# First feed-forward started inside the end of the first attention

## The reference

```python
h = _L0_tok_ref(x, ...)
h = h + _L0_attn_ref(_layernorm(h), wq, wk, wv, wo)      # 16 heads of 64, causal
h = h + _L0_ffn_ref(_layernorm(h), w1, b1, w2, b2)       # 256 -> 1024 -> 256
h = h + _L1_attn_ref(_layernorm(h), Wq, Wk, Wv, Wo, bo)
h = h + _L1_ffn_ref(_layernorm(h), gate_weight, ...)     # 8 experts, all dense
```

```python
h = float2fix(jnp.einsum('bsd,df->bsf', x, w1) + b1, 8)
xq = float2fix(h, 8)
y = jnp.interp(xq, _PWL_X, _PWL_Y)       # 33 points on [-4, 4], GELU exact there
out = jnp.einsum('bsf,fd->bsd', float2fix(y, 8), w2) + b2
return float2fix(out, 8)
```

## Time and profile before

| what | value |
|---|---|
| median of 3 runs | 980.0 us (979.19 to 980.0) |
| profiled execution | 979.99 us, span 978.2 us |
| PE busy | 933.1 us (95%) |
| DVE busy | 579.8 us (59%) |
| ACT busy | 542.0 us (55%) |
| feed-forward of layer 0, first up block to last down projection | 238.3 to 318.7 us |

### The profile page before, as it was taken

How to read it: one execution, slowest core, us unless ns; L and a number is a source line. 1 busy time by engine, 2 the same in 40 slices (tenths; PEclk the granted TensorE clock), 3 DMA queues, 4 the chain that set the end, 5 groups by cost and what they waited for, 6 DMA issues and landing times.

```text
span 978.2 us, 18614 instructions
## 1 busy us (share of the span) xinstructions
PE 933.1 (95%) x7135; PEld 863.7 (88%) x7135; DVE 579.8 (59%) x1251; ACT 542.0 (55%) x1569; POOL 154.8 (16%) x173
## 2 busy tenths in 40 slices
PE   6999999999799999999999899999999999999998
PEld 6877888788677878888889898999999999999998
DVE  5566575746999574665656677555453545444342
ACT  4666464653764664655555526556664647555452
POOL 0332121210000122221210000431110111110111
PEclk9999999999999999999999999999999999999999
DMA  8310000002000210000002011111011111100001
GB/s 325 130 44 2 1 1 1 2 1 87 1 1 1 87 44 1 2 2 1 2 7 81 15 73 44 44 43 46 2 44 44 44 44 44 44 1 1 1 14 38
DMA packets 8796, 34.46 MB, mean 35 GB/s; under 512 B 642, under 2 KB 5122, under 8 KB 5380
## 3 DMA queue, kind: packets, MB, share of 16 engines
q1 hardware_dynamic: 8708, 33.28, 9.4%
HBM read 32.06 MB, written 1.22 MB: 34 GB/s over the span
## 4 chain that ended last, share of the span: by engine, by line
issue 32%; PE 24%; POOL 5%; DVE 5%; ACT 2%; POOLq 0%; DVEq 0%; ACTq 0%
PE D L574 8%; PE O L574 7%; POOL h L362 4%; PE O L740 2%; PE T L726 2%; PE S L715 1%; PE S L574 1%; DVE hid L1528 1%; ACT hid L1100 1%; DVE wslot L1128 1%; PE S L709 1%; POOL h L374 1%; ACT work L1096 1%; PE O L854 1%; POOL vbuf L372 1%
## 5 line engine op out<-in xcount | busy, mean ns | idle before, releaser
L1528 DVE TENSOR_TENSOR hid<-work,hid 128x300 fp32r<-128x300 f32 (+1 forms) x256 | 139.1, 565 | 191.9 <-ACT hid L1100 191.6
L574 PE MATMUL O<-hid,wslot 128*128 128x300 f32 (+3 forms) x1680 | 240.6, 301 | 0.0
L574 PEld LDWEIGHTS O<-hid,wslot 128*128 128x128 f32 x1680 | 233.0, 189 | 0.6
L574 PE MATMUL D<-xn,wslot 128*128 128x300 f32 (+3 forms) x1368 | 222.4, 307 | 1.4 <-ACT hid L1100 1.4
L574 PEld LDWEIGHTS D<-xn,wslot 128*128 128x128 f32 x1368 | 197.7, 189 | 6.1 <-ACT hid L1100 2.7
L1096 ACT ACTIVATE work<-D,prm 128x300 f32<-128x300 f32 (+1 forms) x128 | 66.7, 521 | 179.7 <-PE D L574 179.7
L996 ACT ACTIVATE probs<-S,negmax 111x111 f32<-111x111 f32 (+1 forms) x352 | 117.5, 358 | 53.5 <-DVE negmax L1293 53.2
L553 POOL TENSOR_TENSOR probs<-probs,rsum 111x444 f32<-111x444 f32 (+1 forms) x88 | 80.9, 920 | 379.8 <-DVE rsum L1301 379.8
L574 PE MATMUL S<-xn,wslot 128*128 128x300 f32 (+3 forms) x864 | 136.2, 305 | 0.0
L574 PEld LDWEIGHTS S<-xn,wslot 128*128 128x128 f32 x864 | 125.3, 191 | 0.3
L362 POOL TENSOR_TENSOR h<-h,work 128x300 f32<-128x300 f32 (+1 forms) x56 | 49.5, 905 | 287.6 <-DVE work L1547 287.6
(11 more groups left out here) (174 smaller groups left out, 1165.0 us busy)
## 6 DMA issues: line engine op xcount, KB each, us to landing
raw<-in_moe SPq DMA_DIRECT2D x16, 1024.0 KB, 4.8
raw<-in_attn SPq DMA_DIRECT2D x7, 1024.0 KB, 4.9
work<-in_x SPq DMA_DIRECT2D x2, 1008.0 KB, 8.0
w2f<-in_attn SPq DMA_DIRECT2D x1, 1024.0 KB, 12.6
raw<-in_ffn SPq DMA_DIRECT2D x1, 1024.0 KB, 4.8
w2f<-in_ffn SPq DMA_DIRECT2D x1, 1024.0 KB, 4.9
raw<-in_x SPq DMA_DIRECT2D x2, 504.0 KB, 5.2
out<-h SPq DMA_DIRECT2D x3, 300.0 KB, 2.8
```

The source lines that it names most:

```text
L574: mm = pe.matmul(psum, a, b, start=(first and k == 0), stop=(k == 3 * n - 1))
L1528: nc.vector.tensor_tensor(moe_hid(s, 1), moe_g(s)[:, 0:w], moe_hid(s, 0).bitcast(F32), ALU.subtract).then_inc(m_hid, 1)
```

## The change

TensorE: up blocks 0 and 1 take the places of `keep_busy` in step 22, blocks 2 and 3 that in step 23. Blocks 4 and 5 stand between the two halves of chunk 3's output projection, whose second half now goes to bank T0. The banks of the blocks turn S0, S1, D0, D1 (`BF`). The rest of the blocks follow, with mean and variance of chunk 3 behind blocks 7 and 12, and each half of a down projection by itself behind one pair or more. VectorE: `ff_find(0)` and `ff_part(0)` come in step 22; in the loop `ff_round` is done one pair later; the norm of chunk 3 is centred at p = 3 and finished at p = 9; evictions come by halves. Two quarter splits of each of two weight pieces move. ScalarE: `ff_load` of pair 0 in step 22, and two table loads more, for the root at p = 7.

```diff
+        BF = BS + BD
@@ attention, TensorE
+                    if (l, c, dc) == (0, NC - 1, KD - 1):
+                        pe.wait_ge(t_dve[0], 2 * NUNIT)
+                    else:
+                        take_bank("out", KD * c + dc)
...
                     if u == NUNIT:
-                        keep_busy(*ahead, 6)
+                        if l == 0:
+                            ff_up1(0)
+                        else:
+                            keep_busy(*ahead, 6)
                     if 0 <= u - 1 < NUNIT:
                         transposes(2 * u - 1)
                     if u == NUNIT + 1:
-                        keep_busy(*ahead, 5)
+                        if l == 0:
+                            ff_up1(2)
+                            ff_up1(3)
+                        else:
+                            keep_busy(*ahead, 5)
+                    elif u == NUNIT and l == 0:
+                        ff_up1(1)
...
+                    if l == 0 and u == NUNIT + 1:
+                        ff_up1(4)
+                        ff_up1(5)
                     if due is not None:
                         project_out(due, 1)
@@ feed-forward, TensorE
+            for s in range(6, NC * KH):
+                c, m = s // KH, s % KH
+                ff_up1(s)
+                if (c, m) == (0, KH - 1):
+                    mean(1, 3)
+                if (c, m) == (1, 4):
+                    variance(1, 3)
+                if c >= 1 and m == 5:
+                    ff_down(c - 1, 0)
+                if c >= 2 and m == 1:
+                    ff_down(c - 2, 1)
+                if (c, m) == (NC - 1, 3):
+                    mean(2, 0)
+            variance(2, 0)
+            ff_down(NC - 2, 1)
+            for dc in range(KD):
+                ff_down(NC - 1, dc)
@@ ScalarE
+                    if l == 0 and u == NUNIT:
+                        nc.scalar.preload_act_table_set("gelu_and_others")
+                        ff_load(0)
+                        ff_load(1)
...
+            for p in range(NP):
+                ff_knots(p)
                 if p + 1 < NP:
                     ff_load(2 * p + 2)
                     ff_load(2 * p + 3)
-                if p == -1:
+                if p == 3:
                     square(1, 3)
+                if p == 7:
+                    nc.scalar.preload_act_table_set("natural_log_exp_and_others")
                     inv_root(1, 3)
+                    nc.scalar.preload_act_table_set("gelu_and_others")
@@ VectorE
+                    if l == 0 and NUNIT - 2 <= u < NUNIT:
+                        low_quarter(FIRST_W + W_FF, 3 * (u - (NUNIT - 2)))
                     if u < NUNIT:
                         invert_sums(2 * u)
...
+            for p in range(1, NP + 2):
+                if p <= NP:
                     ff_slope(p - 1)
+                if p >= 2:
+                    ff_round(p - 2)
                 if p < NP:
                     ff_find(p)
+                if p <= NP:
                     ff_line(p - 1)
                 if p < NP:
                     ff_part(p)
+                if p <= NP:
                     ff_sum(p - 1)
-                    ff_round(p - 1)
-                if p == 0:
+                if p == 1:
+                    low_quarter(FIRST_W + 6, 2)
+                    low_quarter(FIRST_W + 6, 3)
+                if p in (1, 2):
+                    add_out(NC - 1, p - 1)
+                if p == 3:
                     center(1, 3)
+                if p == 9:
                     finish(1, 3)
-                if KH <= p < NP and p % (KH // 2) == 0:
-                    ff_out(2 * p // KH - 2)
+                if p in (7, 11, 15):
+                    ff_out1(p // 4 - 1, 0)
+                if p in (10, 14):
+                    ff_out1(p // 4 - 2, 1)
                 if p == 3 * KH // 2:
                     center(2, 0)
-            finish(2, 0)
-            ff_out(NC - 2)
+            root = newton(2, 0)
+            ff_out1(NC - 2, 1)
+            apply(2, 0, root)
             for k in range(SPLITS):
                 low_quarter(FIRST_W + 7, k)
-            ff_out(NC - 1)
+            for dc in range(KD):
+                ff_out1(NC - 1, dc)
```

More of the change, by code:

```diff
@@ L341, in ff_bufs @@
             if p % 3 == 0:
-                flat = vbuf[:, :, :].rearrange("p s n -> p (s n)")
-                three = [pair(flat, k) for k in range(3)]
+                three = [ffs[:, 2 * k:2 * k + 2, :] for k in range(3)]
             elif p % 3 == 1:
@@ L347, in ff_bufs @@
             else:
-                three = [ffs[:, 2 * k:2 * k + 2, :] for k in range(3)]
+                flat = vbuf[:, :, :].rearrange("p s n -> p (s n)")
+                three = [pair(flat, k) for k in range(3)]
             return [t[:, :, 0:w] for t in three]
@@ L813, in _ @@
             attention(0, 0)
[L816 to L834, removed]
-                    if c == 0 and m == 3:
-                        variance(1, 3)
-                    if c >= 2 and m == 1:
-                        ff_down(c - 2)
-                    if c == 2 and m == KH - 1:
-                        mean(2, 0)
-                    if c == NC - 1 and m == KH - 2:
-                        variance(2, 0)
@@ L844, in ff_down @@
-            def ff_down(c):
-                a, w = CHUNKS[c]
-                pe.wait_ge(ff_hid, KH * (c + 1))
-                if c == 0:
-                    pe.wait_ge(w2_in, 16)
-                for dc in range(KD):
-                    if c >= 1:
-                        pe.wait_ge(ff2_ev, KD * (c - 1) + dc + 1)
-                    w2 = w2f[:, :].rearrange("p (a n) -> p a n", n=D)
-                    for i in range(KH):
-                        mm = pe.matmul(BO[dc][:, 0:w], w2[:, i, dc * P:(dc + 1) * P],
-                                       work[:, KH * (c % 2) + i, 0:w], start=(i == 0), stop=(i == KH - 1))
-                    mm.then_inc(ff2_mm, 1)
@@ L1037, in _ @@
             high_part(FIRST_W + 2)
-            attention(0)
             def ff_load(s):
@@ L1056, in ff_knots @@
                 nc.scalar.activation(y1, y1, ACT.Gelu, bias=c_knot1[:, 0:1], scale=1.0 / UNIT).then_inc(ff_y1, 1)
-            for p in range(-1, NP):
-                if p >= 0:
-                    ff_knots(p)
+            attention(0)
+            for p in range(NP):
+                ff_knots(p)
                 if p + 1 < NP:
@@ L1353, in attention @@
                         invert_sums(2 * u + 1)
+                    if l == 0 and u == NUNIT + 1:
+                        break
                     if due is not None:
@@ L1363, in attention @@
                         low_out(u - 1)
+                    if l == 0 and u == NUNIT:
+                        ff_find(0)
+                        ff_part(0)
                     if l == 1 and u == NUNIT + 1:
```

72 lines of the change are left out of this document (47 added, 25 removed).

## The result

| | median us | lowest to highest | executions |
|---|---|---|---|
| before | 980.0 | 979.19 to 981.09 | 4 |
| after | 969.96 | 968.87 to 970.49 | 4 |

The ratio is 0.9895, 95% interval 0.9878 to 0.9913. The forecast was 970.2 us, faster than before.

A forecast was written before the change was run, and what follows sets the result against it. The prediction took VectorE's queue to bound the changed stretch and added its terms: -7.05 up to the last rounding and -2.7 in the tail, -9.8 from 979.99, giving 970.2 us, range 966.8 to 974.3.

The forecast's parts named there:

- The seam (-6.9, +0.3, -1.2): Attention end to feed-forward: VectorE's waits hidden -6.9, first wait grows to 0.9 us, +0.3, two quarter splits moved under cover -1.2.
- One pair, rounding later (-2.8): Feed-forward loop: rounding one pair later makes a wide pair 3.57 instead of 3.76 us; 15 pairs, -2.8 us.
- Rival 2: TensorE becomes the bound; 3 to 5 us of its pauses exposed give 973 to 975 us; chance 0.12.
- the sum for TensorE's queue: TensorE's work after 226.7 us: 73 us, ending at 299.5 without a pause, 7.7 us before the last down projection's forecast end.
- The new waits (+1.1, +0.55, +0.75): Loop: VectorE waits for the last chunk's root +1.1, down projection 0's half +0.55, a half ahead of blocks 30 and 31 +0.75.
- an unbroken chain: VectorE before the change: five waits at the seam, 0.38 to 2.38 us, then work without a break.
- rival 6: Slower through the clock: TensorE at 0.50 after a pause; one episode nothing to 1 us more, seven give 981; chance 0.04.
- Up to the last rounding: All terms from 226.7 us to the feed-forward's last rounding: -7.05 us, so it starts at 301.7 instead of 308.8.
- The tail (-4.4, +1.7): After the last rounding: last down projection waits less, -4.4; third block of the next layer waits for bank O1, +1.7.
- The half eviction (+1.15): VectorE: one half of chunk 2's evictions now stands before the last rounding, +1.15 us.
- The sum: Whole kernel: -7.05 up to the last rounding and -2.7 in the tail, -9.8 us, giving 970.2 us.
- sign of being wrong by the clock: Profile after: the prediction is wrong if the granted clock is 0.5 for more than one episode.

The follow-up runs named there:

- Kernel 10: Changed kernel with up blocks 0 to 5 started late again, VectorE's first find and part behind normalisation, splits and additions; 975.98 us, ratio 0.9952.
- kernel 1: Changed kernel with each rounding put back right behind its own sum; 970.51 us, ratio 0.9899 against the kernel before.
- kernel 2: Kernel before the change with only the rounding done one pair later; 980.0 us, ratio 0.9992.
- kernel 6: Changed kernel with the four quarter splits of the key weights behind chunk 3's evictions; 969.58 us, ratio 0.9897 against the kernel before.
- kernel 5: Changed kernel without the two table loads in the loop, chunk 3's root replaced by a scaled copy; 968.7 us, ratio 0.9893 against the kernel before.
- kernel 9: Changed kernel with six products of constants in TensorE's pause before chunk 3's mean; 969.23 us, ratio 0.9886 against the kernel before.
- kernel 12: Changed kernel with key-weight splits behind chunk 3's evictions, down projection 2's first half behind the last up block, six constant products in TensorE's pause; 968.05 us.
- kernel 4: Changed kernel with down projections whole again and each chunk's evictions together; 970.79 us, ratio 0.9899 against the kernel before.
- kernel 7: Kernel before the change with only chunk 2's evictions moved ahead of the next layer's root; 980.96 us, ratio 1.0007.
- kernel 11: Changed kernel with key-weight splits behind chunk 3's evictions and down projection 2's first half behind the last up block; 968.57 us, ratio 0.9883.
- kernel 8: Changed kernel with key-weight splits behind chunk 3's evictions, down projection 2's first half behind the last up block, chunk 3's mean two blocks later; 969.31 us.

## Why the prediction was right, by its steps

**The seam (-6.9, +0.3, -1.2): right.** Slope 0 was forecast at 235.6, with the later start at 236.4, and is at 236.44; the first wait is 0.92 (forecast 0.9). Kernel 10 gives 4.95 for the start alone, and the forecast for that part is 6.9 less the root's 2.38, 4.5. That the two splits stay hidden (-1.2) was not tried by itself, but rows bear it out: from the first mark to VectorE's wait of 0.58, with the second split in between, it is 6.58 us in both kernels (220.08 to 226.66 and 220.88 to 227.46).

**One pair, rounding later (-2.8): the row right, the term not.** A pair takes 3.56 as forecast. But kernels 1 and 2, one for each kernel, show the order alone to be worth 0.64 and 0.59. This is the step that failed as a cause: the gain was priced as if VectorE alone set the end. TensorE was near enough to take 2.66 of 3.31 back as waits. Rival 2's mechanism, TensorE as the bound inside the loop, holds (51.52 of 52.97 us busy), without its price of 3 to 5 us. What hid it was the sum for TensorE's queue, 73 us with 7.7 to spare: from 226.80 to 307.50 TensorE was busy for 77.35 of 80.70 us, so 3.35 were idle, 1.81 of them the pause at 243. About 1.4 of the 4.3 us more are the fall of the clock: to the start of the first half down projection it is 33.47 from the first mark, in kernel 6, less its wait of 0.81, 32.07.

**The new waits (+1.1, +0.55, +0.75): sizes nearly right.** The prediction calls VectorE's loop before "an unbroken chain", which misses one wait:

```profile
302.17 0.55 DVE L1403 TENSOR_TENSOR probs<-probs,probsT 128x372 f32<-128x372 f32 x1 [1.06 <-ACT probs L1056]
```

The sum kept it by leaving it as it was. With it the forecast is 1.10 + 0.55 + 0.75 + 1.06 = 3.46 of waits; measured are 1.20, 0.94, 0.69 and 0.63, also 3.46. Slope 8's is the table loads' (kernel 5). Find 7's is larger by 0.39, and where the clock did not fall it is 0.46 to 0.48 (kernels 6, 9, 12). So rival 6's one episode, "nothing to 1 us more", was there and cost about 0.46. That the total is the same to a hundredth is luck: without the fall of the clock it would have been 0.46 less. The term for the rounding and these terms were one thing told twice, once as a gain and once as a loss; the sum came out since both were counted.

**Up to the last rounding:** forecast -7.05, measured 81.19 - 88.72 = -7.53. The 0.5 between them has the size of what the order of roundings saved beyond the forecast, 3.31 of queue and not 2.8; which pairs save more was not looked into.

**The tail (-4.4, +1.7): right.** From the last rounding to the first block of the second layer it was 9.89 and is 307.50 - 302.07 = 5.43: -4.46. From there to the second mark it was 327.01 - 318.69 = 8.32 and is 317.37 - 307.50 = 9.87: +1.55 against +1.7, with the pause of 1.24 ahead of the third block in it (kernel 6, without the pause, is 1.35 shorter). Together -2.91 against -2.7. The halves are 1.29 of that, and 1.62 comes without them (kernel 4); the evictions moved in the kernel before lose (kernel 7). The half eviction (+1.15) is the price of the halves in VectorE's queue; at the same clock they cost 0.40 up to the last rounding.

**The sum:** forecast -9.8, measured -10.44 by the marks, -10.0 by the medians. The prediction's sign of being wrong by the clock, more than one episode at 0.50, did not come within the feed-forward: there it was one, as before.

**Is there more to have?** Kernel 12 is at 968.05 us against 969.96; the intervals of the two ratios overlap. By the marks it is 2.60 shorter, of which 1.35 is the tail and 1.25 the loop; of the loop's, 0.77 is the half's move and the rest, 0.48, has the size of the clock's part. Its span is 966.0 against 968.7.

## What to carry to other kernels

A sum over one engine's queue can give the right total for wrong reasons: as soon as a shortened queue comes near a second one, add up that one's busy time too, and price a saving only at the places where the second waits for the first. An experiment that puts a start back must put back the order behind it as well, or it measures one long wait (8.47 us) for everything queued behind it. A pause that is moved is not hidden; look where it ends up, and what runs at half clock behind it. And differences of half a microsecond are read only between profiles in which the clock did the same: whole projections looked 0.85 better and were 0.40.

## What was unexpected of the hardware

The clock does not fall behind a pause each time. Behind the same wait of 1.81 us it was granted at 0.50 from 247 to 248 us in the changed kernel and in kernels 5 and 11, and at 1.00 in kernels 4 and 6, all with the same instructions up to there. The kernel before fell to 0.50 behind its wait of 2.23 us in its profile, and not in all of its executions: of 21 executions on one chip six had a mean granted clock of 1.000, with spans of 977.7 to 978.9 us, and seven had 0.995, with spans of 978.6 to 982.9 us. The granted 0.50 is 1.2 GHz, 1.00 is 2.4. The wait at find 7 was 0.46 to 0.48 where the clock stayed up, 0.82 and 0.94 where it fell on up blocks (kernel 11 and the changed kernel), and 2.16 where it fell on the half down projection (kernels 8 and 10). In the second layer the same work took 650.5 to 650.9 us behind the second mark where the clock stayed up from 530 to 560 us, 651.2 to 651.6 where its mean was 0.83 over one window of ten us (in kernel 10 0.91 and 0.92 over two), and 653.2 to 653.4 where it was 0.67 or 0.71 over one and 0.99 or 0.95 over the next. What decides whether it falls stays open.
